# Gathering the low bits of the feed-forward weights in the projection phase instead of in attention

## The reference

```python
xq = _rms_norm(x @ wq.T, q_norm_w, EPS)
xk = _rms_norm(x @ wk.T, k_norm_w, EPS)
xv = x @ wv.T
...
scores = jnp.einsum('bhtd,bhsd->bhts', xq, xk) * scale + bias[None]
attn = jax.nn.softmax(scores, axis=-1)
...
g = jnp.einsum('th,ih->ti', xf, gate_w) * gate_s
u = jnp.einsum('th,ih->ti', xf, up_w) * up_s
hdn = jax.nn.silu(g) * u
out = jnp.einsum('ti,hi->th', hdn, down_w) * down_s
...
x = x + _layernorm(_L0_attn_ref(_layernorm(x, axis=-1), ...), axis=-1)
x = x + _layernorm(_L0_ffn_ref(_layernorm(x, axis=-1), ...), axis=-1)
```

## Time and profile before

| | before |
|---|---|
| median of 3 runs | 1285.86 us (1285.02 to 1287.29) |
| time of the profiled execution | 1284.65 us |
| its span | 1282.9 us |
| PE busy | 1200.5 us (94%) |
| DVE busy | 910.8 us (71%) |
| ACT busy | 750.8 us (59%) |
| POOL busy | 386.0 us (30%) |
| granted PE clock, mean over the span | 0.986 |

### The profile page before, as it was taken

How to read it: one execution, slowest core, us unless ns; L and a number is a source line. 1 busy time by engine, 2 the same in 40 slices (tenths; PEclk the granted TensorE clock), 3 DMA queues, 4 the chain that set the end, 5 groups by cost and what they waited for, 6 DMA issues and landing times.

```text
span 1282.9 us, 29210 instructions
## 1 busy us (share of the span) xinstructions
PE 1200.5 (94%) x9016; PEld 1014.4 (79%) x9016; DVE 910.8 (71%) x2386; ACT 750.8 (59%) x1629; POOL 386.0 (30%) x460
## 2 busy tenths in 40 slices
PE   5999999997999899999999999999979979999998
PEld 4868778785777788888888898889867768888876
DVE  4597776867999788788888878788854355646364
ACT  3645455554999797777777777777732234232330
POOL 1000000001689675443445435443421100202021
PEclk9999999998999899999999999999989989999999
DMA  4216263455566565454555455454442252111110
GB/s 165 98 74 247 103 242 131 181 197 191 202 252 236 175 198 181 154 176 145 177 166 187 145 174 165 160 169 151 151 153 105 98 186 70 66 34 66 34 66 34
DMA packets 99259, 189.34 MB, mean 148 GB/s; under 512 B 8032, under 2 KB 36832, under 8 KB 99168
## 3 DMA queue, kind: packets, MB, share of 16 engines
q1 hardware_dynamic: 99168, 188.21, 43.1%
HBM read 116.54 MB, written 71.63 MB: 147 GB/s over the span
## 4 chain that ended last, share of the span: by engine, by line
PE 80%; DVE 9%; issue 4%; ACT 3%; DMA 3%; POOL 1%; DVEq 0%; SPq 0%; ACTq 0%; POOLq 0%
PE bank L1248 18%; PE bank L1379 17%; PE bank L1316 15%; PE bank L1270 10%; PE bank L1279 10%; PE bank L1297 2%; PE bank L1295 2%; PE bank L1296 2%; PE bank L1305 2%; DVE inv_rms L988 2%; DMA q_st<-q_scr 1%; DVE pT_lo L1041 1%; DVE oT_lo L1053 1%; DVE raw L967 1%; DMA w_stage<-wqT 1%
## 5 line engine op out<-in xcount | busy, mean ns | idle before, releaser
L826 ACT ACTIVATE p_sb<-u_sb,low 128x384 f32<-128x384 f32 (+2 forms) x512 | 274.4, 536 | 54.2 <-DVE low L1034 47.4
L1034 DVE CUSTOM_DVE_ANT_0 u_sb<-bank,bias 128x384 f32<-128x384 f32 (+2 forms) x512 | 231.3, 452 | 56.5 <-PE bank L1270 36.0
L1041 DVE TENSOR_TENSOR pT_lo<-bank,pT_hi 128x384 f16<-128x384 f32 (+2 forms) x512 | 232.3, 454 | 36.8 <-ACT pT_hi L833 21.4
L1270 PE MATMUL bank<-k_st,q_st 128*128 128x384 f32 (+2 forms) x1024 | 249.0, 325 | 7.3 <-DMA q_st<-q_scr 3.0
L833 ACT ACTIVATE pT_hi<-bank 128x384 f16<-128x384 f32 (+2 forms) x512 | 206.6, 403 | 68.5 <-PE bank L1279 64.8
L1279 PE MATMUL bank<-ident,p_sb 128*128 128x128 f32 x1152 | 219.0, 281 | 21.8 <-DVE pT_lo L1041 15.3
L1270 PEld LDWEIGHTS bank<-k_st,q_st 128*128 128x128 f32 x1024 | 176.5, 192 | 31.8 <-DVE v_out L1008 3.3
L1279 PEld LDWEIGHTS bank<-ident,p_sb 128*128 128x128 f32 x1152 | 137.9, 141 | 60.3 <-ACT p_sb L826 40.7
L583 POOL TENSOR_TENSOR rstd<-var_eps,minus_half 128x1 f32<-128x1 f32 (+1 forms) x31 | 23.4, 753 | 482.7 <-DVE var_eps L929 482.7
L1295 PE MATMUL bank<-v_st,pT_hi 128*128 128x65 f16 x1152 | 158.4, 193 | 0.5 <-DVE pT_lo L1041 0.5
L1296 PE MATMUL bank<-v_st,pT_hi 128*128 128x64 f16 x1152 | 158.7, 194 | 0.0
(11 more groups left out here) (115 smaller groups left out, 2324.2 us busy)
## 6 DMA issues: line engine op xcount, KB each, us to landing
q_scr<-qk SPq DMA_DIRECT2D x64, 512.0 KB, 2.7
q_st<-q_scr SPq DMA_DIRECT2D x32, 1024.0 KB, 7.8
k_st<-k_scr SPq DMA_DIRECT2D x64, 256.0 KB, 3.1
o_scr<-o_out SPq DMA_DIRECT2D x128, 128.0 KB, 2.5
o_in<-o_scr SPq DMA_DIRECT2D x16, 1024.0 KB, 5.1
k_scr<-qk SPq DMA_DIRECT2D x16, 512.0 KB, 3.1
z_in<-z_scr SPq DMA_DIRECT2D x8, 1024.0 KB, 5.9
v_scr<-v_out SPq DMA_DIRECT2D x4, 1040.0 KB, 5.9
```

Source lines behind the costliest of these rows:

```text
L826: nc.scalar.activation(p_sb[:, u % RING, 0:w], u_sb[:, u % RING, 0:w], ACT.Exp, scale=-1.0, bias=low[:, u % RING:u % RING + 1]).then_inc(p ...
L1034: nc.vector.tensor_tensor_reduce(out=u_sb[:, u % RING, 0:w], in0=bank[u % 2][:, 0:w], in1=bias[:, 2 * u // UNITS, u % REP, at:at + w], sca ...
L1041: nc.vector.tensor_tensor(pT_lo[:, u % RING, 0:w], bank[2 + u % 2][:, 0:w], pT_hi[:, u % RING, 0:w], ALU.subtract).then_inc(pT_ready, 1)
L1270: mm = nc.tensor.matmul(bank[u % 2][:, 0:w], q_st[:, s, r, P * i:P * i + P], k_st[:, s, part, P * key:P * key + w], start=(part == 0), sto ...
```

## The change

The gathering moves from attention to projection. `BITS_AT` now names nine products, n = 8 to 11 and 13 to 17; behind the square of each, DVE gathers one piece. In the first batch only the last six of the nine slots are used (two groups of three), in each of the other batches all nine, which makes 33. SP loads a piece two slots ahead of its use, one transfer for each slot, into the buffer of its part, with a semaphore for each of the three parts; the load waits for the gathering of the piece that was in the buffer before it. `count_bits` moves from the start of the tail to behind the gathering at n = 17 of the last batch. The buffers `f_bits` and `used_bits` move to the memory of the projection phase (a filler, `spare2`, keeps the addresses in attention), and the two small tiles of the count live throughout.

```diff
-BITS_AT = (19, 20, 21)
+BITS_AT = (8, 9, 10, 11, 13, 14, 15, 16, 17)
+BIT_GROUPS = INTER // P
+AHEAD = 2
...
+def bits_at(b, k):
+
+    group, part = len(BITS_AT) // PARTS * b + k // PARTS, k % PARTS
+    group = group - (len(BITS_AT) // PARTS * B - BIT_GROUPS)
+    if isinstance(group, int) and not 0 <= group < BIT_GROUPS:
+        return None
+    return group, part
...
+            def load_bits(group, part):
+
+                at_least(sp, bits_ready, PARTS * (group - 1) + part + 1)
+                hold(sp)
+                flat = (gateT, upT, downT)[part].rearrange("(p a) n -> p (a n)", p=P).rearrange("p (k c) -> k p c", c=D)
+                sp.dma_start(f_bits[:, part], flat[bass.ds(group, 1)].rearrange("a p c -> p (a c)")).then_inc(bits_loaded[part], DMA)
...
                 for kind, n in SCHEDULE:
+                    if kind == "gemm" and n in BITS_AT:
+                        k = BITS_AT.index(n) + AHEAD
+                        if isinstance(b, int) and b == 0 and k == PARTS:
+                            load_bits(0, 0)
+                        elif bits_at(b, k):
+                            load_bits(*bits_at(b, k))
...
-                    load_bits(t)
...
+            def gather_bits(group, part):
+
+                dve.wait_ge(bits_loaded[part], DMA * (group + 1))
+                at_least(dve, bits_ready, PARTS * group + part)
+                hold(dve)
+                new, used = (a.bitcast(mybir.dt.int32) for a in (f_bits[:, part], used_bits[:]))
+                if isinstance(group, int) and group == 0 and part == 0:
+                    nc.vector.tensor_copy(used, new).then_inc(bits_ready, 1)
+                else:
+                    nc.vector.tensor_tensor(used, used, new, ALU.bitwise_or).then_inc(bits_ready, 1)
...
+                        if n in BITS_AT and bits_at(b, BITS_AT.index(n)):
+                            gather_bits(*bits_at(b, BITS_AT.index(n)))
+                        if last and n == BITS_AT[-1]:
+                            count_bits()
...
-                    if tile is not None and u in BITS_AT:
-                        gather_bits(tile, BITS_AT.index(u))
...
-            count_bits()
             for k in range(LAG):
                 finish_tile(k)
```

More of the change, by code:

```diff
@@ L215, in sandwich_layer @@
         slopes = sb(ctx, "slopes", [P, H + 4 * REP])
+        lo_count = sb(ctx, "lo_count", [P, 1])
+        lo_total = sb(ctx, "lo_total", [1, 1])
         with ExitStack() as s1:
@@ L231, in sandwich_layer @@
             norm_w = sb(s1, "norm_w", [P, QC + KVC])
+            f_bits = sb(s1, "f_bits", [P, PARTS, D])
+            used_bits = sb(s1, "used_bits", [P, D])
             with ExitStack() as before_norms:
@@ L254, in sandwich_layer @@
             o_out = sb(s2, "o_out", [P, TT, REP, HD])
-            f_bits = sb(s2, "f_bits", [P, PARTS, D])
-            used_bits = sb(s2, "used_bits", [P, D])
+            sb(s2, "spare2", [P, PARTS + 1, D])
             wo_stage = sb(s2, "wo_stage", [P, TT, D])
@@ L280, in sandwich_layer @@
             y_s = sb(s4, "y_s", [P, TT, D])
-            lo_count = sb(s4, "lo_count", [P, 1])
-            lo_total = sb(s4, "lo_total", [1, 1])
             hid = sb(s4, "hid", [P, T])
@@ L317, in sandwich_layer @@
             "y_stats y_moments y_var y_rstd y_normed z_ready z_stored")
-        bits_loaded, bits_ready, bits_masked, lo_counted, lo_summed = sems(
-            "bits_loaded bits_ready bits_masked lo_counted lo_summed")
+        bits_loaded = sems("bits_loaded0 bits_loaded1 bits_loaded2")
+        bits_ready, bits_masked, lo_counted, lo_summed = sems("bits_ready bits_masked lo_counted lo_summed")
         f_loaded = sems("f_loaded0 f_loaded1")
@@ L447, in load_wo @@
                              .rearrange("a p c d -> p (a c) d")).then_inc(wo_loaded, DMA)
[L449 to L455, removed]
             def store_late(n, first, end):
@@ L976, in norm, with count_bits @@
                     split_raw(b, f)
+            def gather_bits(group, part):
[7 more added lines that the diff above has]
+                    nc.vector.tensor_tensor(used, used, new, ALU.bitwise_or).then_inc(bits_ready, 1)
+            def count_bits():
+                dve.wait_ge(bits_ready, PARTS * BIT_GROUPS)
+                low = used_bits[:].bitcast(mybir.dt.int32)
+                nc.vector.tensor_scalar(low, low, LOW_BITS, None, ALU.bitwise_and).then_inc(bits_masked, 1)
+                dve.wait_ge(bits_masked, 1)
+                nc.vector.tensor_reduce(lo_count[:], low, mybir.AxisListType.X, ALU.max).then_inc(lo_counted, 1)
             def project(b, last=False):
@@ L1061, in norm_y @@
                 layer_norm(t, y_n[:], acc[:], 0, y_rstd, y_normed)
[L1063 to L1072, removed]
             def unit_work(n, u):
@@ L1119, in split_piece @@
                 nc.vector.tensor_tensor(lo, src, hi.bitcast(F32), ALU.subtract).then_inc(f_ready, 1)
[L1121 to L1127, removed]
             def finish_tile(k):
```

## The result

| | before | changed |
|---|---|---|
| median, 16 runs each on one chip | 1283.76 us (1280.21 to 1287.29) | 1287.26 us (1284.42 to 1292.18) |
| ratio | | 1.0026, 95% interval 1.0016 to 1.0037 |
| time of the profiled execution | 1284.65 us | 1288.33 us |
| its span | 1282.9 us | 1286.5 us |
| granted PE clock, mean | 0.986 | 0.988 |

What follows compares the result with a forecast made beforehand. PE was taken as the bound, busy 1200.5 of 1282.9 us. Attention, later batches and count 0, first batch +2.3 and tail -0.2 gave +2.1 on 1285.86: 1288.0 us, range 1285.4 to 1290.2.

Steps and rivals of the forecast that it cites:

- the first batch's +0.9: First projection batch, lower bound: statistics at 57.5 us and the fifth piece landing in time give +0.9 us.
- The likeliest class: Whole kernel: no change beyond 0.2% (2.6 us) got chance 0.52, slower 0.41, faster 0.07.
- Attention, 0: Attention: taking out ORs and loads gains 0 us, since PE is the bound there and waits for no load.
- The faster rival: Attention: DVE's lateness carries to the `pT_lo` waits; half of 11.4 us gone gives 1282.3 us; chance 0.08.
- Batches two to four, 0: Later projection batches: ORs fit DVE's idle time; late loads may push DVE by some tenths; 0 us.
- The slower-still rival: Batches two to four: late loads make PE wait up to 1 us in each; +5, 1291 us; chance 0.07.
- The count in the last batch, 0: Last projection batch: OR, mask and maximum take 2.1 us against 2.94 us idle before n = 18; 0 us.
- The first batch, +2.3: First projection batch: copy delays statistics, fifth piece's late load delays the reciprocal; PE's second batch 2.3 us late.
- the rule weighed there: First-batch loads: one queue's descriptors start in order but may overlap; start order gives 2.1 us in sum, full overlap 3.5.
- Half clock, a rival at 0.25: First batch: PE's longer idle time triggers half clock, up to 1.6 us more; total +3.7, 1289.6 us; chance 0.25.
- The tail, -0.2: Tail: PE restarts 1.5 us earlier but then waits for the split behind `z_in`'s statistics; -0.2 us, bounds -0.5 and +0.5.

Runs made afterwards that it cites:

- the five profiles that have both waits: Four profiles of the changed kernel, and one of it with two count-like operations put back at the tail's start (ratio 1.0027); mean first-batch loss 3.2 us.
- the first five of the table: Profiles of the kernel before, of it with three pieces in attention (0.9997), and of the changed kernel with first-batch gathering absent (1.000), early (1.0004), or three ORs without waits (0.9994).
- the one with three ORs: Changed kernel with first-batch pieces loaded early, three gathered at n = 3, 4, 7 and three at n = 15, 16, 17: 1284.26 us, ratio 0.9994.
- the first repeat: The changed kernel, unchanged, profiled once more: 1284.44 us.
- the kernel with the early gathering: Changed kernel with the first batch's six pieces loaded between weight blocks and gathered at n = 3, 4, 7, 8, 10, 11: 1284.03 us, ratio 1.0004.

## Why the prediction came out as it did

The order and the place were right. The median of 1287.26 us is nearer to the forecast 1288.0 than the mechanism deserves: the base was 1285.86 us, the median of three runs, and with 16 runs it is 1283.76. That the base came out 2.1 us too high and the difference 1.3 too low, and that the two partly cancel, is luck. What counts is the difference, +2.1 forecast and +3.4 measured, which is just above the forecast's own range of +0.9 to +3.3. (The lower end should have been +0.7: the first batch's +0.9 and the tail's -0.2.) The likeliest class had been no measurable change; at 0.26% the result lies just on the slower side of that line, which its interval straddles.

*Attention, 0:* right. Waits for `pT_lo` 11.3 us against 11.4; with 30 pieces taken from the kernel before, 0.9997. The faster rival fell with it. One reading was off: the waits stand about a dozen units behind the last gathering, 21 us (630.47 to 651.73 us in the kernel before), and not 30.

*Batches two to four, 0:* right in the sum, not in the detail. "Some tenths" of lateness were nine waits of up to 2.2 us, 11.3 us in all. The third batch still starts 3.3 us late, as the second does, since DVE's idle 4.75 us before n = 17 take that up and PE waits for squares four products old. The slower-still rival saw the late loads and overrated them.

*The count in the last batch, 0:* right. The mask took 0.43 us there where it took 0.89 in the tail, so the cover was larger than assumed.

*The first batch, +2.3:* the mechanism was right and the size was low: 3.0 us in the first profile (17.00 against 13.99 to the reciprocal), 2.4 to 3.0 in all at full clock. The copy delayed the statistics by 5.51 - 4.27 = 1.24 us from the sum of n = 11, where 1.26 was forecast. That it fits so closely is partly luck: x itself lands sooner or later, and the distance is 5.2 to 5.6 us in the five profiles that have both waits, and 4.2 to 4.6 in the first five of the table, about 1.0 less. By the rule weighed there (the Trainium skill, "DMA: Bandwidth & Descriptors", "Two DMAs through the same engine are not ordered") full overlap would have put the piece at 59.1; by that rule's order of starts, it comes just behind x, and the trace agrees with the order: x 8.0 us after its issue at 49.47, the first piece at 58.2, the next two at about 58.8 and 59.4. The rest of the difference, 0.7 us, is two small terms: the fifth piece took 3.3 us to land and not 2.8, and the stretch from the statistics to the sum of n = 13 took 6.15 us and not 5.99. That ORs cost only where they have used up the idle time was right: three of them without a wait cost nothing, and the prediction's lower bound of +0.9, four ORs and the copy with every piece in time, is what the estimate of 0.8 us above comes to.

*Half clock, a rival at 0.25:* it is real, and as priced. Idle time grew from 1.62 to 2.2 us (2.4 forecast), the half clock costs 1.6 us, and two profiles of seven have it. It was set up as another case, all or nothing for a kernel; it is a term that comes and goes between executions of the same program, and should have stood in the forecast with its share, 0.25 x 1.6 = 0.4 us by the prediction's own chance. The Trainium skill's page "TensorE: Matmul & The Clock Gate", section "What's actually happening", says that the windows in which activity is looked at run free of the kernel; the trace agrees, with full clock after 2.19 and 2.24 us of idle time and half clock after 2.24 and 2.22.

*The tail, -0.2:* right, and for the reason given. From the transposes (936.72 us before, 940.84 after) the wait for that tile's last split ends 16.4 us later in the kernel before and 16.3 in the changed one, since `z_in` gates it. Two other kernels without the count in the tail bear it out. In the one with nothing gathered in the first batch and in the one with three ORs, PE fell to half clock behind these transposes all the same and came to this wait 1.6 us later; the wait was 3.08 and 2.79 us in place of 4.78, and it ended 16.2 and 15.9 us behind the transposes. Here is the first of the two, whose transposes start at 937.73:

```profile
953.88 0.79 PE L1332 MATMUL bank<-wo_hi,oT_hi 128*128 128x512 f32 x1 [3.08 <-DVE oT_lo L1091]
```

The early restart at full clock, where it comes, is paid back by the longer wait behind it. From the transposes to the first wait for `hid` it is 297.4 us before and 297.0, 297.4, 296.7 and 298.3 in the four profiles of the changed kernel. With the count put back the ratio does not move.

What stays open is the rest of the spread, some microseconds between executions: the stretch from the second batch to the transposes took 838.8 to 842.9 us in the four profiles of the changed kernel, with no difference in the waits for `pT_lo`. The loads of `q_st` came later in some (a wait of 3.35 us at 435.72 in the first profile, with half clock behind it, and 0.7 in all in the first repeat) and the clock had other dips. It is not of the change: the kernel before has such a wait of 2.83 us at 431.92, with half clock behind it too, and took 842.1 us for the stretch, and the kernel with the early gathering 838.7. Its causes were not tried.

## What to carry to other kernels

Work that fits into idle time is free only if its input is there: three ORs of 0.6 us cost nothing, while a gathering that waited for its piece, with other work queued behind it, cost 1.2 us ahead of the statistics and 1.6 ahead of the reciprocal (each with the time of the operation itself). And count the slots: by the rows a fourth OR ahead of the reciprocal was 0.5 us more than the idle time there could hold. Place the load first, then the operation, and never put one that waits for a transfer ahead of one that is due. A ring of buffers ties the load of the fifth piece to the use of the second, so slots close together need an earlier start, which was shown here, or more buffers, which was not tried. When PE's idle time grows by half a microsecond, add the price of a half clock times its share of the executions, and profile the same program several times before reading a microsecond from one.

## What the runs showed of the hardware

- In the first batch, idle times of 2.2 us let PE restart at 1.2 GHz in two of seven profiles and at 2.4 GHz in five, with 1.6 us in none of seven (the kernels of the table and those with `z_in`'s statistics later).
- The AND of 128 x 512 int32 took 0.43 us at 294 us and 0.89 us at 937.89 us. On another tile at the second place (941.25 us, the kernel with the count in the tail) it took 0.89 us again, so it is the place and not the tile. POOL was idle in the first place and busy through the whole of the second, which was not tried as a cause; the OR took 0.66 to 0.69 in projection and attention alike.
- A load of 256 KB took 2.7 to 3.3 us when the queue was short, and 8.1 us (from 50.09 to 58.2) behind 2 MB. Three of them issued one behind the other there landed 0.6 us apart.
- In the tail a shorter idle time did it too: in the ten profiles without the count there, PE idled 0.97 or 0.98 us ahead of the first matmul for `oT_lo`, behind the transposes that open the tail, and then ran at 2.4 GHz in eight (granted clock 1.00 from 941 to 947 us in the changed kernel's first profile) and at 1.2 GHz in two (0.50 from 940 to 942 us in the kernel with nothing gathered in the first batch).
